# A decoder block on one NeuronCore: attention to the context and its two norms moved into the recurrence's program, batch by batch

## The reference

```python
def _layernorm(x, axis=-1, eps=1e-05):
    m = jnp.mean(x, axis=axis, keepdims=True)
    v = jnp.var(x, axis=axis, keepdims=True)
    return (x - m) / jnp.sqrt(v + eps)
...
def _L0_xattn_ref(query, key, value, Wq, bq, Wk, bk, scale_factor, dropout_p):
    q = jnp.einsum('bld,ed->ble', query, Wq) + bq
    k = jnp.einsum('bld,ed->ble', key, Wk) + bk
    scores = jnp.einsum('bqd,bkd->bqk', q, k) / jnp.float32(scale_factor)
    attn = jax.nn.softmax(scores, axis=-1)
    return jnp.einsum('bqk,bkd->bqd', attn, value)
...
    x = x + _L0_attn_ref(_layernorm(x, axis=-1), ...)        # the recurrence (RWKV-6)
    x = x + _L0_xattn_ref(_layernorm(x, axis=-1), ctx_1024, ctx_1024, ...)
    x = x + _L0_ffn_ref(_layernorm(x, axis=-1), ...)         # its own attention, an MLP, 8 experts
```

## Time and profile before

| quantity | value |
|---|---|
| median of 3 runs | 1265.61 us |
| profiled execution: its own time, its span | 1263.1 us, 1261.4 us |
| TensorE, VectorE, ScalarE busy | 1117.4, 804.6, 741.0 us |
| mean granted TensorE clock | 0.948 |
| recurrence's last addition to x ends | 116.6 us |
| first matmul of the feed-forward's attention | 172.7 us |

### The profile page before, as it was taken

How to read it: one execution, slowest core, us unless ns; L and a number is a source line. 1 busy time by engine, 2 the same in 40 slices (tenths; PEclk the granted TensorE clock), 3 DMA queues, 4 the chain that set the end, 5 groups by cost and what they waited for, 6 DMA issues and landing times. The chain is left out here.

```text
span 1261.4 us, 35646 instructions
## 1 busy us (share of the span) xinstructions
PE 1117.4 (89%) x14748; PEld 568.3 (45%) x14748; DVE 804.6 (64%) x1296; ACT 741.0 (59%) x1459; POOL 346.0 (27%) x673
## 2 busy tenths in 40 slices
PE   6997779888889999689999999999978786899996
PEld 2442344333324443256766766766745333222221
DVE  4894246877753333147777776776735555999985
ACT  5312363777744444356676776766745372799994
POOL 0552021333325433134323233332304333100000
PEclk9998676999999999799999999999999996899999
DMA  4000016111014330160021021010010004311100
GB/s 192 1 0 1 0 46 219 41 47 47 16 36 101 72 62 1 53 117 8 8 15 13 8 18 10 8 12 7 8 10 1 1 11 137 127 47 42 41 16 34
DMA packets 134479, 51.61 MB, mean 41 GB/s; under 512 B 103904, under 2 KB 126448, under 8 KB 133680
## 3 DMA queue, kind: packets, MB, share of 16 engines
q1 hardware_dynamic: 134284, 49.32, 16.5%
q10 hardware_dynamic: 36, 0.02, 0.0%
HBM read 33.12 MB, written 15.81 MB: 39 GB/s over the span
## 5 line engine op out<-in xcount | busy, mean ns | idle before, releaser
L2230 DVE TENSOR_REDUCE re_nmax<-ps 128x1 f32<-128x512 f32 x256 | 158.9, 683 | 88.3 <-PE ps L1998 88.3
L2141 ACT ACTIVATE normed<-ps,re_nmax 128x512 f32<-128x512 f32 x256 | 158.8, 688 | 89.6 <-DVE re_nmax L2230 89.6
L2019 PE MATMUL ps<-const,normed 128*128 128x128 f32 x1024 | 145.1, 281 | 7.8 <-ACT normed L2141 5.0
L1049 DVE TENSOR_REDUCE ga_nmax<-ps 128x2 f32<-128x1024 f32 x128 | 147.1, 1216 | 6.8 <-PE ps L805 6.8
L953 ACT ACTIVATE ga_pt<-ps 128x512 f32<-128x512 f32 x256 | 139.2, 598 | 16.3 <-PE ps L841 15.4
L2019 PEld LDWEIGHTS ps<-const,normed 128*128 128x128 f32 x1024 | 108.8, 141 | 36.3 <-ACT normed L2141 24.7
L1049 DVE TENSOR_REDUCE da_nmax<-ps 128x2 f32<-128x256 f32 (+3 forms) x128 | 101.9, 819 | 33.4 <-PE ps L816 32.5
L953 ACT ACTIVATE da_pt<-ps 128x512 f32<-128x512 f32 (+3 forms) x256 | 96.9, 436 | 44.0 <-PE ps L841 41.8
L1479 DVE TENSOR_TENSOR ex_u<-ps,ex_s 128x512 f32<-128x512 f32 x48 | 32.8, 690 | 98.7 <-PE ps L1344 75.8
L2147 ACT ACTIVATE re_pT<-ps 128x512 f32<-128x512 f32 x128 | 76.3, 597 | 28.4 <-PE ps L2019 20.6
L2250 DVE COPY re_pT<-ps 128x512 f32<-128x512 f32 x128 | 82.2, 684 | 10.8 <-PE ps L2019 10.1
(11 more groups left out here) (395 smaller groups left out, 2007.3 us busy)
## 6 DMA issues: line engine op xcount, KB each, us to landing
ex_gates<-gates_scratch SPq DMA_DIRECT2D x4, 2048.0 KB, 14.6
da_qst<-da_stacks SPq DMA_DIRECT2D x32, 96.0 KB, 2.2
da_kst<-da_stacks SPq DMA_DIRECT2D x32, 96.0 KB, 2.3
ga_qst<-ga_stacks SPq DMA_DIRECT2D x32, 96.0 KB
ga_kst<-ga_stacks SPq DMA_DIRECT2D x32, 96.0 KB
da_stacks<-da_qkparts SPq DMA_DIRECT2D x6, 384.0 KB, 3.3
ga_stacks<-ga_qkparts SPq DMA_DIRECT2D x6, 384.0 KB, 2.9
weights<-in_weights SPq DMA_DIRECT2D x1, 2048.0 KB, 7.5
```

What stands on the lines that cost most here:

```text
L1049: nc.vector.tensor_reduce(nmax[:, u % 2, :, pr, qt], g.ps[:, 2 * (step % S_GROUPS):2 * (step % S_GROUPS) + 2, 0:keys_of(qt)], AX.X, ALU.ma ...
L2019: last = nc.tensor.transpose(g.ps[:, bank_of("tile", s, idx), bass.ts(kt, 128)], p[:, QUAD_ORDER[idx], bass.ts(kt, 128)], g.c("ident"))
L2141: nc.scalar.activation(p[:, QUAD_ORDER[idx], :], g.ps[:, S_BANK + QUAD_ORDER[idx], :], ACT.Exp, bias=nmax[:, s % 2, idx:idx + 1]).then_inc ...
L2230: nc.vector.tensor_reduce(nmax[:, s % 2, idx:idx + 1], g.ps[:, S_BANK + quad, :], AX.X, ALU.max, negate=True).then_inc(maxed, 1)
```

## The change

The functions `norm_stage`, `xattn_stage` and `bf_constants` are gone. Their work is a class `cross_attention` with one method per step and batch, and these steps stand in the recurrence's own lists, in the same Block. Batch b uses the PSUM banks 2b ("even") and 2b+1 ("odd"): centred x, scores and weighted values in the even bank; means, queries, transposed weights and the next norm's centred x in the odd one. Key making and the first two `center` steps sit inside the loop over n; all else follows the loop, the batches one behind the other. The softmax works on a batch's four tiles (128 x 128 elements an instruction). The three casts stand at the start of VectorE's list. Its tensors reuse those of the recurrence; `normed` takes the place of `rw_o` and `ff_xn` that of `rw_xv`.

```diff
-def norm_stage(nc, g, tag, source, out, center, mean, chunks=B, width=T):
...
-def rwkv_stage(nc, g):
+def rwkv_stage(nc, g, o, xv):
...
+        CONTEXT_KEYS_AT, CROSS_CENTER_AT = NSCAN + 1, {NSCAN + 2: 0, NSCAN + 3: 1}
+        cross = cross_attention(nc, g, sem, sb, scanned, added, added_x, NSCAN, mix, eu, vsb, dx[:, 0, :], xv)
...
+                    if n == CONTEXT_KEYS_AT:
+                        cross.keys(pe)
+                    if n in CROSS_CENTER_AT:
+                        cross.center(pe, CROSS_CENTER_AT[n])
+                cross.mean(pe, 0)
                 center(B - 1)
+                cross.mean(pe, 1)
+                cross.center(pe, 2)
                 mean(B - 1)
+                cross.queries(pe, 0)
+                cross.queries(pe, 1)
+                cross.mean(pe, 2)
+                cross.scores(pe, 0)
+                cross.scores(pe, 1)
                 output(B - 1)
+                cross.queries(pe, 2)
+                cross.turn(pe, 0)
+                cross.center(pe, 3)
+                cross.scores(pe, 2)
+                cross.mean(pe, 3)
+                cross.attend(pe, 0)
+                cross.turn(pe, 1)
+                cross.turn(pe, 2)
+                cross.next_center(pe, 0)
+                cross.queries(pe, 3)
+                cross.attend(pe, 1)
+                cross.scores(pe, 3)
+                cross.next_mean(pe, 0)
+                cross.next_center(pe, 1)
+                cross.attend(pe, 2)
+                cross.turn(pe, 3)
+                cross.next_mean(pe, 1)
+                cross.attend(pe, 3)
+                cross.next_center(pe, 2)
+                cross.next_center(pe, 3)
+                cross.next_mean(pe, 2)
+                cross.next_mean(pe, 3)
...
+                for b in range(B - 1):
+                    square_centered(b)
+                    inverse_root(b)
+                cross.copy_keys(act)
+                cross.square(act, 0)
+                cross.square(act, 1)
+                cross.root(act, 0)
+                square_centered(B - 1)
+                cross.root(act, 1)
+                cross.square(act, 2)
+                inverse_root(B - 1)
+                cross.copy_queries(act, 0)
+                cross.copy_queries(act, 1)
+                cross.root(act, 2)
...
+                dve.wait_ge(g.const_loaded, 16)
+                for to, name in ((g.ident_bf, "ident"), (g.lowered_bf, "lowered"), (g.loweredT_bf, "loweredT")):
+                    nc.vector.tensor_copy(to[:, :], g.c(name)).then_inc(g.cast, 1)
...
+                cross.scale(dve, 0)
+                cross.scale(dve, 1)
                 gate(B - 1)
+                cross.lower(dve, 0)
+                cross.scale(dve, 2)
+                cross.weigh(dve, 0)
                 take(B - 1)
...
-def xattn_stage(nc, g):
...
+                cross.lower(dve, 1)
+                cross.weigh(dve, 1)
+                cross.lower(dve, 2)
+                cross.weigh(dve, 2)
+                cross.add(dve, 0)
+                cross.scale(dve, 3)
+                cross.add(dve, 1)
+                cross.lower(dve, 3)
+                cross.weigh(dve, 3)
+                cross.next_scale(dve, 0)
+                cross.add(dve, 2)
+                cross.add(dve, 3)
+                cross.next_scale(dve, 1)
+                cross.next_scale(dve, 2)
+                cross.next_scale(dve, 3)
+
...
+class cross_attention:
...
+        self.xn, self.q, self.sq = mix[:, :, 0, :], mix[:, :, 1, :], mix[:, :, 2, :]
+        self.p = p.rearrange("p (n c) -> p n c", c=LC)
+        self.pt = pt[0:LC, :, :]
...
+    def keys(self, pe):
+        nc, g = self.nc, self.g
+        pe.wait_ge(g.weights_loaded[1], 16)
+        pe.wait_ge(g.ctx_loaded, 32)
+        pe.wait_ge(self.scanned, self.scans - 2)
+        nc.tensor.matmul(self.odd(0)[:, 0:B * LC], g.w("xk"), g.ctxT[:, :], start=True, stop=True)\
+            .then_inc(self.k_made, 1)
+
+    def center(self, pe, b):
+        if b < 2:
+            pe.wait_ge(self.scanned, self.scans)
+        pe.wait_ge(self.added_x, b + 1)
+        if b == 2:
+            pe.wait_ge(self.added_heads, B)
+        self.nc.tensor.matmul(self.even(b), self.g.c("center"), self.x(b), start=True, stop=True)\
+            .then_inc(self.centered, 1)
...
+    def mean(self, pe, b):
+        pe.wait_ge(self.squared, b + 1)
+        if b == 0:
+            pe.wait_ge(self.k_ready, 1)
+        self.nc.tensor.matmul(self.odd(b), self.g.c("mean"), self.sq[:, b, :], start=True, stop=True)\
+            .then_inc(self.averaged, 1)
...
+    def turn(self, pe, b):
+        pe.wait_ge(self.weighed, b + 1)
+        for t in range(QT):
+            last = self.nc.tensor.transpose(self.odd(b)[0:LC, bass.ts(t, 128)], self.p[:, QT * b + t, :],
+                                            self.g.c("ident"))
+        last.then_inc(self.turned, 1)
+
+    def attend(self, pe, b):
+        pe.wait_ge(self.pt_ready, b + 1)
+        self.nc.tensor.matmul(self.even(b), self.g.ctx[:, b, :], self.pt[:, b, :], start=True, stop=True)\
+            .then_inc(self.attended, 1)
+
...
+    def next_center(self, pe, b):
+        pe.wait_ge(self.added, b + 1)
+        self.nc.tensor.matmul(self.odd(b), self.g.c("center"), self.x(b), start=True, stop=True)\
+            .then_inc(self.n_centered, 1)
+
+    def next_mean(self, pe, b):
+        pe.wait_ge(self.n_squared, b + 1)
+        self.nc.tensor.matmul(self.even(b), self.g.c("mean"), self.sq[:, b, :], start=True, stop=True)\
+            .then_inc(self.n_averaged, 1)
...
+    def lower(self, dve, b):
+        nc, n = self.nc, self.tiles(b)
+        dve.wait_ge(self.scored, b + 1)
+        nc.vector.tensor_reduce(self.nmax[:, n], self.score_tiles(b), AX.X, ALU.max, negate=True)\
+            .then_inc(self.maxed, 1)
+        dve.wait_ge(self.maxed, b + 1)
+        nc.vector.tensor_tensor(self.p[:, n, :], self.score_tiles(b),
+                                self.nmax[:, n].unsqueeze(2).broadcast_to([128, QT, LC]), ALU.add)\
+            .then_inc(self.lowered, 1)
+
+    def weigh(self, dve, b):
+        nc, n = self.nc, self.tiles(b)
+        dve.wait_ge(self.exped, b + 1)
+        nc.vector.tensor_reduce(self.total[:, n], self.p[:, n, :], AX.X, ALU.add).then_inc(self.totalled, 1)
+        dve.wait_ge(self.totalled, b + 1)
+        nc.vector.reciprocal(self.total[:, n], self.total[:, n]).then_inc(self.inverted, 1)
+        dve.wait_ge(self.inverted, b + 1)
+        nc.vector.tensor_tensor(self.p[:, n, :], self.p[:, n, :],
+                                self.total[:, n].unsqueeze(2).broadcast_to([128, QT, LC]), ALU.mult)\
+            .then_inc(self.weighed, 1)
...
-def ffn_stage(nc, g, y):
+def ffn_stage(nc, g, xn, y):
...
-def bf_constants(nc, g):
...
-        rwkv_stage(nc, g)
-        xattn_stage(nc, g)
-        bf_constants(nc, g)
         with ExitStack() as inner:
             normed = inner.enter_context(nc.sbuf_tensor("normed", [D, B, T], fp32))
-            ffn_stage(nc, g, normed)
+            with nc.sbuf_tensor("ff_xn", [D, B, T], fp32) as ff_xn:
+                rwkv_stage(nc, g, normed, ff_xn)
+                ffn_stage(nc, g, ff_xn, normed)
```

More of the change, by code:

```diff
@@ L477, in _ @@
                         take(TAKE_AT[n])
+                cross.scale(dve, 0)
+                cross.scale(dve, 1)
                 gate(B - 1)
+                cross.lower(dve, 0)
+                cross.scale(dve, 2)
+                cross.weigh(dve, 0)
                 take(B - 1)
-def xattn_stage(nc, g):
[L484 to L546, removed]
-                dve.wait_ge(maxed, 1)
-                nc.vector.tensor_tensor(p[:, :, :], scores, nmax[:, :].unsqueeze(2).broadcast_to([128, NTILE, LC]),
-                                        ALU.add).then_inc(lowered, 1)
-                dve.wait_ge(exped, 1)
-                nc.vector.tensor_reduce(total[:, :], p[:, :, :], AX.X, ALU.add).then_inc(totalled, 1)
-                dve.wait_ge(totalled, 1)
-                nc.vector.reciprocal(total[:, :], total[:, :]).then_inc(inverted, 1)
-                dve.wait_ge(inverted, 1)
-                nc.vector.tensor_tensor(p[:, :, :], p[:, :, :],
-                                        total[:, :].unsqueeze(2).broadcast_to([128, NTILE, LC]), ALU.mult)\
-                    .then_inc(normed, 1)
-                for b in range(B):
-                    dve.wait_ge(attended, b + 1)
-                    nc.vector.tensor_tensor(g.x[:, bass.ts(b, T)], g.ps[:, b, :], g.x[:, bass.ts(b, T)],
-                                            ALU.add).then_inc(added, 1)
@@ L2686, in grouped_stage @@
                         classes=rows_dram, front=front)
-def bf_constants(nc, g):
-    with nc.Block() as block:
-        @block.vector
-        def _(dve):
-            dve.wait_ge(g.const_loaded, 16)
-            for to, name in ((g.ident_bf, "ident"), (g.lowered_bf, "lowered"), (g.loweredT_bf, "loweredT")):
-                nc.vector.tensor_copy(to[:, :], g.c(name)).then_inc(g.cast, 1)
```

105 lines of the change are left out of this document (100 added, 5 removed).

## The result

The changed kernel takes 1233.8 us (median of 4 runs, 1231.52 to 1235.33), against 1265.44 us before: ratio 0.9753, interval 0.9719 to 0.9786. The forecast was 1231.5 us, range 1225 to 1244. The profiled execution took 1231.52 us with a span of 1229.8; the forecast's sum for it had been 1230.9.

What follows compares the result with a forecast made beforehand. TensorE, half of the stretch at the low clock, plus pauses between phases was taken as the bound; 1263.1 - 32.2 = 1230.9 us against the profiled execution, forecast 1231.5 us, range 1225 to 1244.

Steps and rivals of the forecast that it cites:

- TensorE's work and gaps, 33.9 + 0.9 us: From the recurrence's end through the second norm: 33.9 us of TensorE work at the high clock plus 0.9 us of gaps.
- What follows the last mean: End of the second norm: last two roots, 1.3 us each, and a 0.69 us product, complete at 139.4 us.
- the starting row: The forecast's start at 101.98 us, where TensorE had just waited 0.92 us for GpSimd's product.
- Small softmax pieces, 0.30 us: VectorE's softmax instructions of 128 elements in the attention, taken at 0.30 us each, between bounds of 0.28 and 0.69.
- Barrier, 1.11 us: Semaphore clearing and barrier between second norm and next stage, taken at 1.11 us against 0.74 before, costing 0.4 us.
- The next stage's start: First matmul of the feed-forward's attention, forecast at 140.5 in place of 172.7 us, 32.2 us sooner.
- rival 4: Next stage's low-clock stretch starts elsewhere in its list; each 3 us is 1.3 us, either way; inside the forecast's 0.76.
- the price: In the next stage, each further microsecond at the low clock was said to lose 0.43 us.
- Rival 1: Clock falls within the new recurrence-to-second-norm stretch; if at 120 us and staying, 1245 us; chance 0.11.
- Rival 2: Hand-offs bind in place of TensorE if every softmax piece costs 0.69 us; 7.1 us later, 1238 us; chance 0.09.
- Rival 3: Low clock covers the whole stretch, gaining 1.6 us only (1261.5), and lengthens the next stage's low stretch; chance 0.03.
- The walk: Stepping through the three engines' new lists with trace durations: TensorE ends at 136.8 us, second norm complete at 139.4.

Runs made afterwards that it cites:

- e3: The changed kernel with each of the first norm's four mean matmuls issued twice on TensorE; 1234.5 us, ratio 0.9783.
- e9: The changed kernel with the squares and the mean matrix of the two norms in bf16; 1230.7 us, ratio 0.9749.
- e11: The changed kernel with three of each batch's five softmax pieces on VectorE done twice; 1231.5 us, ratio 0.9759.
- e8: The changed kernel with the three casts again in a Block of their own before the feed-forward's attention; 1233.0 us, ratio 0.9761.
- e7: The changed kernel with one unused 512-column matmul in each of steps 9 to 12 of the feed-forward's attention; 1233.0 us, ratio 0.9759.
- e1: The changed kernel with the same instructions in the same Block, but ordered phase by phase over all batches; 1243.2 us, ratio 0.9847.
- e10: The changed kernel with each of the first norm's four squares on ScalarE done twice; 1234.3 us, ratio 0.9783.
- e4: The changed kernel with each of the first norm's four products on VectorE done twice; 1229.3 us, ratio 0.9736.
- e2: The kernel before the change with unused matmuls put into TensorE's pauses; 1257.3 us, ratio 0.9964.
- e12: The changed kernel with bf16 squares and mean, reordered steps and three unused matmuls before the feed-forward's attention; 1229.0 us, ratio 0.9739.

## Why the prediction was right

- *TensorE's work and gaps, 33.9 + 0.9 us.* From 101.68 to 136.57 us: 34.9. e3 shows that work added to TensorE is on the path; e9 shows that the hand-offs stand close behind. VectorE worked 18.0 and ScalarE 22.1 us of this (19 and 24 forecast).
- *What follows the last mean.* The second norm is complete at 139.06 us, 37.4 us after the starting row, as forecast (101.98 to 139.4).
- *Small softmax pieces, 0.30 us.* Measured 0.29 and 0.28; exponentials 0.31 where I took 0.34. They were covered in the changed kernel, but e11 shows that 0.6 of any more would not be.
- *Barrier, 1.11 us.* 1.13 us (139.06 to 140.19). The casts' Block was worth 0.8 (e8).
- *The next stage's start.* 140.19 against 140.5 us; the tail fell by 32.2 us, the figure forecast.
- *What I undervalued.* The median is 2.3 us over the forecast, within the range. Part is where I set the sum: against the profiled execution, 2.5 us under the median of its runs, and then only 0.6 us higher. Against the median it would have been 1233.4 us. I also gave nothing to the stage behind. Its low stretch is 3.4 us longer, as in rival 4, and the rest 0.9 us; but the changed kernel's two profiles differ by 0.9 us there too, and e7 does not bear out the price, so this part is not shown.
- *Rivals.* Rival 1 did not come in the changed kernel, but the clock fell within the tail in e1, e9 and e10. Rival 2 did not come, as its condition, 0.69 us a piece, was 0.29; e4 and e11 show that the hand-offs are partly on the path all the same. Rival 3, the whole tail at the low clock, came in no run, and none was made to test it. For single low stretches half of TensorE's work was about right as a price (e10; e2 with the fillers' delays taken out).
- *Luck.* The walk's 0.1 us is better than the method: in e3, e4, e8, e9, e11 and e12 the expected and the measured change of the tail differ by up to 0.8 us, and by 1.7 and 3.9 us in e10 and e1, where the clock fell.

The gain was not one thing. Of 32.2 us, the common Block with phases, clock included, is 19.7 (e1), and the batches one behind the other add 12.5. The clock runs through both: alone, all else as before, it gives 9.0 us with the fillers in the way (e2), and some 14 by the estimate without them.

## What to carry to other kernels

Where phases of a few microseconds leave each engine idle in turn, sum the busiest engine's work at its full clock and walk the new lists with durations of the old trace: that came within 0.1 us here, and within 0.8 us in the experiments in which the clock stayed up or fell late; where it fell early, the walk was up to 3.9 us short. A filler in a pause must end before the next real work is ready, or it eats what it gives (e2, e7). Then ask what stands right behind the new bound, since adding to it costs all and taking from it gives little until the order follows. Below 0.3% judge such a change by a stretch of the profile, which repeated to 0.1 us in the two profiles of the changed kernel, not by the whole time.

## What the runs showed of the hardware

The same code behind the tail took 1084.3 to 1094.9 us in these profiles, and the clock fell at other places in each: in the changed kernel it was low for 86 us of the rest, in its repeat 97 us, in e2 107 us. The two go together only in part (correlation about 0.7 over all fourteen profiles).

In e10 the clock fell at 124.1 us; TensorE's one pause before that was 0.51 us long and ended at 121.95 us. In the changed kernel, with the same kinds of matmul and no pause from 116 to 133 us, it stayed up.
